# A graph network on one core: norms woven into the products around them

## The reference, cut to what matters

```python
x = _layernorm(x + _L0_gnn_ref(x, ...), axis=-1)   # two GCN convolutions
x = _layernorm(x + _L1_gnn_ref(x, ...), axis=-1)   # seg. means over dst and over src, then a GRU cell
x = _layernorm(x + _L2_gnn_ref(x, ...), axis=-1)   # three dense layers on [x, summed edge_attr, u], leaky relu
x = _layernorm(x + _L3_gnn_ref(x, ...), axis=-1)   # two SAGE convolutions
```

## Time and profile before

| | us |
|---|---|
| median of 3 runs | 1084.41 (1082.30 to 1086.23) |
| the profiled execution, its own time | 1082.45 |
| its span, first to last instruction | 1080.8 |
| mean granted PE clock in it | 0.938 |
| PE busy | 955.1 |
| DVE busy | 618.8 |
| ACT busy | 483.5 |
| POOL busy | 67.1 |

### The profile page before, as it was taken

How to read it: one execution, slowest core, us unless ns; L and a number is a source line. 1 busy time by engine, 2 the same in 40 slices (tenths; PEclk the granted TensorE clock), 3 DMA queues, 4 the chain that set the end, 5 groups by cost and what they waited for, 6 DMA issues and landing times.

```text
span 1080.8 us, 19631 instructions
## 1 busy us (share of the span) xinstructions
PE 955.1 (88%) x7324; PEld 831.5 (77%) x7324; DVE 618.8 (57%) x905; ACT 483.5 (45%) x787; POOL 67.1 (6%) x134
## 2 busy tenths in 40 slices
PE   7469999997799999759989899899699599999993
PEld 6469999997799799749978788544344399969982
DVE  3669999995544555645554455354623545415544
ACT  0135445444655566375557567322322523233311
POOL 1200000000000000200003244100000000000000
PEclk9989999999899999959989999899689689999997
DMA  9767777774000000000000000000000000000001
GB/s 268 140 148 170 169 164 170 162 168 99 2 0 0 1 1 0 20 0 0 0 2 0 0 1 0 1 1 8 17 0 1 0 1 0 1 1 1 0 0 60
DMA packets 168662, 48.00 MB, mean 44 GB/s; under 512 B 154948, under 2 KB 167268, under 8 KB 168593
## 3 DMA queue, kind: packets, MB, share of 16 engines
q1 hardware_dynamic: 155462, 44.96, 18.1%
q10 hardware_dynamic: 12012, 0.83, 0.8%
q0 software_dynamic: 1120, 1.29, 0.5%
HBM read 45.44 MB, written 8.02 MB: 49 GB/s over the span
## 4 chain that ended last, share of the span: by engine, by line
PE 82%; DVE 6%; ACT 4%; DMA 3%; issue 2%; SPq 2%; ACTq 0%; DVEq 0%
PE bank L1393 17%; PE bank L1394 16%; PE bank L1336 11%; PE bank L1326 7%; PE bank L1488 4%; PE bank L1481 4%; PE bank L1489 3%; PE bank L1564 2%; PE bank L1527 2%; DMA lists_d<-in_src 2%; ACT wb L715 2%; PE bank L1553 2%; PE bank L1528 2%; DVE tmp L1010 1%; PE bank L1552 1%
## 5 line engine op out<-in xcount | busy, mean ns | idle before, releaser
L1393 PE MATMUL bank<-stage,f_hi 125*128 125x392 f32 x1000 | 348.1, 348 | 36.9 <-DVE f_lo L1054 21.3
L1394 PE MATMUL bank<-stage,f_lo 125*128 125x392 f32 x1000 | 345.8, 346 | 0.0
L1393 PEld LDWEIGHTS bank<-stage,f_hi 125*128 125x128 f32 x1000 | 192.0, 192 | 40.0 <-issue 23.3
L949 DVE CAST stage<-counts 125x2352 fp32r (+1 forms) x120 | 165.4, 1381 | 97.4 <-PE bank L1394 97.0
L1394 PEld LDWEIGHTS bank<-stage,f_lo 125*128 125x128 f32 x1000 | 191.9, 192 | 0.0
L688 ACT ACTIVATE stage<-counts 125x1568 fp32r x80 | 107.7, 1346 | 179.2 <-PE bank L1394 179.2
L1336 PE MATMUL bank<-tmp,wb 128*65 128x25 f32 x2000 | 130.3, 219 | 8.3 <-DVE tmp L901 8.3
L1336 PEld LDWEIGHTS bank<-tmp,wb 128*65 128x65 f32 x2000 | 127.1, 142 | 8.5 <-DVE tmp L901 8.5
L632 ACT ACTIVATE counts<-bank 125x500 uint8<-125x500 f32 x188 | 87.0, 536 | 43.4 <-PE bank L1326 42.9
L753 ACT ACTIVATE stage<-bank 125x500 fp32r<-125x500 bf16 x150 | 87.6, 588 | 37.4 <-PE bank L1481 29.1
L878 DVE TENSOR_TENSOR xT<-xT,tmp 128x2560 bf16<-128x2560 bf16 (+1 forms) x63 | 92.8, 1473 | 1.2 <-ACT rowb L612 1.2
(11 more groups left out here) (196 smaller groups left out, 972.4 us busy)
## 6 DMA issues: line engine op xcount, KB each, us to landing
wb<-in_edge_attr SPq DMA_DIRECT2D x125, 256.0 KB, 3.6
lists_d<-in_dst SPq DMA_DIRECT2D x1, 3104.0 KB
lists_d<-in_src SPq DMA_DIRECT2D x1, 3104.0 KB
wa<-in_x SPq DMA_DIRECT2D x1, 1562.5 KB
out<-wb SPq DMA_DIRECT2D x6, 250.0 KB
xT<-in_dst SPq DMA_DIRECT2D x63, 4.0 KB, 3.3
xT<-in_dst ACTq DMA_DIRECT2D x62, 4.0 KB, 3.0
wb<-in_L_gnn_w_ih SPq DMA_DIRECT2D x1, 384.0 KB, 3.6
```

Source lines behind the costliest of these rows:

```text
L949: nc.vector.tensor_copy(set_buffer(u, m), counts[:, SETS[u][0]:sum(SETS[u]), chunk(pair * 2 + off)]).then_inc(s["set_d_ready"], 1)
L1393: mm(bank[h][:, 0:CH], f_hi[:, first + k, :], rhs[:, k, :], start=(first + k == 0), stop=False)
L1394: last = mm(bank[h][:, 0:CH], f_lo[:, first + k, :], rhs[:, k, :], start=False, stop=(first + k == HI - 1))
```

## The change

Norm 0 is written out piece by piece: ACT widens sets 1 and 3 of sum 2's first chunk between the groups, DVE scales groups 4 to 6 and widens set 4 before its last low parts. DVE squares `rowb`, a chunk at a time, inside sum 2; POOL's squaring is gone. Sums 2 and 3 are written out without loops on ACT and DVE.

The gates use one bank each (0 to 3), and PE waits for each bank's reader in the chunk before. Norm 1 has three parts (groups 0 to 2, 3 and 4, 5 and 6). Its groups are transposed from banks 4 to 6 behind gate chunks 2, 3, 4, 6 and 7 and between the first layer products; all go back through bank 7 and ACT. The layers' products use banks 0 and 1, 2 and 3, and 4. Norm 2, also in three parts, begins behind layer chunk 2. L2's weights but `l2w2` move to `wl3` and are loaded when L3's were; `l2w2` is loaded when the gate products that read its place are done; L3's weights follow the last result. The statistics of norms 1 and 2 have a small tensor of their own, `n_small`.

```diff
-        NORM_BANK = ((2, 3, 4, 5, 6, 7, 1), (0, 1, 2, 3, 4, 5, 6), (0, 1, 2, 3, 4, 5, 6), (0, 1, 4, 5, 6, 7, 2))
-        BACK_BANK = ((4, 5, 6, 7, 4, 5, 6), (7, 0, 1, 2, 3, 4, 5), (4, 5, 6, 7, 4, 5, 6))
...
+        NORM_BANK = ((2, 3, 4, 5, 6, 7, 1), (4, 5, 6, 4, 5, 6, 5), (5, 6, 7, 5, 6, 7, 2), (0, 1, 4, 5, 6, 7, 2))
+        BACK_BANK = ((4, 5, 6, 7, 4, 5, 6), (7, 7, 7, 7, 7, 7, 7), (4, 5, 6, 7, 4, 5, 6))
+        PARTS_OF = ((0, 2, NGR), (0, 3, 5, NGR), (0, 3, 5, NGR), (0, 4, NGR))
+        ACT_SCALES = ((0, 1, 2, 3), (0, 1, 2), (3, 4), (0, 2, 4, 6))
...
             sp.wait_ge(s["y_made"], NC)
+            sp.dma_start(l2w1x, p["L2_gnn_w1"][0:D, :]).then_inc(s["l2w_in"], 16)
+            sp.dma_start(l2w1a, p["L2_gnn_w1"][D:D + DE, :]).then_inc(s["l2w_in"], 16)
+            sp.dma_start(l2w1u, p["L2_gnn_w1"][D + DE:256, :]).then_inc(s["l2w_in"], 16)
+            sp.dma_start(l2w3, p["L2_gnn_w3"].rearrange("(k p) n -> p k n", k=2)).then_inc(s["l2w_in"], 16)
+            sp.wait_ge(s["gates_done"], 4 * NC - 2)
+            sp.dma_start(l2w2, p["L2_gnn_w2"].rearrange("(k p) n -> p k n", k=2)).then_inc(s["l2w_in"], 16)
+            sp.wait_ge(s["l2_y"], NC)
...
-            pool.wait_ge(s["norm_t"], NGR)
-            nc.gpsimd.tensor_tensor(rowb[:, :], rowb[:, :], rowb[:, :], ALU.mult).then_inc(s["rowb_sq"], 1)
...
-            norm_to_sources(0, 2)
-            neighbour_sum(2)
+            deviations(0, 0)
+            scaled(0, 0)
+            high_part(0, 0)
+            scaled(0, 1)
+            high_part(0, 1)
+            widen_set(2, 0, 0, 1)
+            deviations(0, 1)
+            scaled(0, 2)
+            high_part(0, 2)
+            scaled(0, 3)
+            high_part(0, 3)
+            high_part(0, 4)
+            widen_set(2, 0, 0, 3)
+            high_part(0, 5)
+            high_part(0, 6)
+            rest_of_sum(2, ((0, 0, 1), (0, 0, 3)))
...
+                act.wait_ge(s["gates_done"], 4 * c + 1)
                 if c >= 1:
                     act.wait_ge(s["gate_y"], c)
+                nc.scalar.activation(tmp[:, 0, :], bank[0][:, 0:CH], ACT.Sigmoid, bias=cols[:, C_BR:C_BR + 1]).then_inc(s["gate_r"], 1)
+                act.wait_ge(s["gates_done"], 4 * c + 2)
+                nc.scalar.activation(tmp[:, 1, :], bank[1][:, 0:CH], ACT.Sigmoid, bias=cols[:, C_BZ:C_BZ + 1]).then_inc(s["gate_z"], 1)
+                if c == 6:
+                    scaled(1, 0)
+                    scaled(1, 1)
+                if c == 7:
+                    scaled(1, 2)
+                    keep_back(1, 0)
                 act.wait_ge(s["gate_t"], c + 1)
                 nc.scalar.activation(tmp[:, 3, :], tmp[:, 2, :], ACT.Tanh, bias=cols[:, C_BIH + 2:C_BIH + 3]).then_inc(s["gate_n"], 1)
+                if c == 5:
+                    deviations(1, 0)
             nc.scalar.activation(small[:, 0:1], mean_w[:, :], ACT.Sqrt)
...
+            act.wait_ge(s["bu_made"], 1)
+            keep_back(1, 1)
+            hidden(0, 0)
+            keep_back(1, 2)
             deviations(1, 1)
...
+            for c in range(NC):
+                if c + 1 < NC:
+                    hidden(0, c + 1)
+                if 1 <= c <= 4:
+                    keep_back(1, c + 2)
+                if c == 6:
+                    deviations(2, 0)
+                if c == 7:
+                    high_part(2, 0)
+                    high_part(2, 1)
+                hidden(1, c)
+                if c == 0:
+                    deviations(1, 2)
+            high_part(2, 2)
+            deviations(2, 1)
+            act.wait_ge(s["l2_y"], NC)
+            widen_set(3, 0, 0, 1)
+            scaled(2, 3)
+            high_part(2, 3)
+            deviations(2, 2)
+            scaled(2, 4)
+            high_part(2, 4)
+            widen_set(3, 0, 0, 3)
+            high_part(2, 5)
+            high_part(2, 6)
+            rest_of_sum(3, ((0, 0, 1), (0, 0, 3)))
...
+            def neighbour_sum(q, dest, more=None, then=None, unrolled=False, first_last=True, squared=False):
...
+                    c = pair * 2 + off
+                    if squared:
+                        nc.vector.tensor_tensor(rowb[:, chunk(c)], rowb[:, chunk(c)], rowb[:, chunk(c)], ALU.mult).then_inc(s["rowb_sq"], 1)
+                        dve.wait_ge(s["rowb_sq"], c + 1)
                     dve.wait_ge(s["set_d_used"], pair * 6 + (24 * q + 3 * off + 3 + 2))
...
+                        if first_last or h or not isinstance(pair, int) or pair:
+                            conv(q, pair, h, 4)
...
+                if unrolled:
+                    for t in range(NC // 2 - 1):
...
+            statistics(0, 0)
+            statistics(0, 1)
+            variances(0, 0)
+            statistics(0, 2)
+            statistics(0, 3)
+            scales(0, 0)
+            for k in (4, 5, 6):
+                statistics(0, k)
+            variances(0, 1)
+            low_part(0, 2, 0)
+            conv(2, 0, 0, 2)
+            low_part(0, 2, 1)
+            scales(0, 1)
+            scaled(0, 4)
+            low_part(0, 2, 2)
+            scaled(0, 5)
+            scaled(0, 6)
+            low_part(0, 2, 3)
+            conv(2, 0, 0, 4)
+            for k in (4, 5, 6):
+                low_part(0, 2, k)
...
+            neighbour_sum(2, wa, unrolled=True, first_last=False, squared=True)
...
             for c in range(NC):
+                dve.wait_ge(s["gates_done"], 4 * c + 3)
                 dve.wait_ge(s["gate_r"], c + 1)
+                nc.vector.scalar_tensor_tensor(tmp[:, 2, :], bank[3][:, 0:CH], cols[:, C_BHH + 2:C_BHH + 3], tmp[:, 0, :], ALU.add, ALU.mult).then_inc(s["gate_h"], 1)
+                if c in (3, 4, 5):
+                    statistics(1, c - 3)
+                if c == 5:
+                    variances(1, 0)
+                    dve.wait_ge(s["l2_bias"], 1)
+                    nc.vector.tensor_tensor(cols[:, C_L2BU:C_L2BU + 2], cols[:, C_L2B1:C_L2B1 + 2], bank[7][:, 0:2], ALU.add).then_inc(s["bu_made"], 1)
+                if c == 6:
+                    scales(1, 0)
+                if c == 7:
+                    statistics(1, 3)
+                dve.wait_ge(s["gates_done"], 4 * c + 4)
+                dve.wait_ge(s["gate_h"], c + 1)
+                nc.vector.tensor_tensor(tmp[:, 2, :], tmp[:, 2, :], bank[2][:, 0:CH], ALU.add).then_inc(s["gate_t"], 1)
...
+            statistics(1, 4)
+            variances(1, 1)
             leaky(0, 0)
+            scales(1, 1)
+            scaled(1, 3)
+            statistics(1, 5)
+            scaled(1, 4)
+            leaky(0, 1)
             for c in range(NC):
+                if c >= 1 and c + 1 < NC:
                     leaky(0, c + 1)
+                if c == 0:
+                    statistics(1, 6)
+                    variances(1, 2)
+                if c in (3, 4, 5):
+                    statistics(2, c - 3)
+                if c == 5:
+                    variances(2, 0)
+                if c == 6:
+                    scales(2, 0)
+                    scaled(2, 0)
+                    scaled(2, 1)
+                if c == 7:
+                    scaled(2, 2)
+                    low_part(2, 3, 0)
+                    low_part(2, 3, 1)
+                    statistics(2, 3)
+                    statistics(2, 4)
+                    variances(2, 1)
                 leaky(1, c)
+                if c == 0:
+                    scales(1, 2)
+                    scaled(1, 5)
+                    scaled(1, 6)
+                if c in (1, 2):
+                    conv(3, 0, 0, 2 * c - 2)
                 dve.wait_ge(s["l2_y"], c + 1)
...
+            low_part(2, 3, 2)
+            scales(2, 1)
+            statistics(2, 5)
+            statistics(2, 6)
+            variances(2, 2)
+            low_part(2, 3, 3)
+            scales(2, 2)
+            scaled(2, 5)
+            scaled(2, 6)
+            conv(3, 0, 0, 4)
+            for k in (4, 5, 6):
+                low_part(2, 3, k)
+            neighbour_sum(3, wa, unrolled=True, first_last=False)
...
+                earlier = [b for b in range(k) if NORM_BANK[i][b] == NORM_BANK[i][k]]
+                if earlier:
+                    wait_scaled(pe, i, earlier[-1])
...
+                if c:
+                    pe.wait_ge(s["gate_r"], c)
+                input_gates(c, 0)
+                if c:
+                    pe.wait_ge(s["gate_z"], c)
+                input_gates(c, 1)
+                if c:
+                    pe.wait_ge(s["gate_h"], c)
+                mm(bank[3][:, 0:CH], wt["whh2"], xT[:, chunk(c)], start=True, stop=True).then_inc(s["gates_done"], 1)
+                if c:
+                    pe.wait_ge(s["gate_t"], c)
+                input_gates(c, 2)
+                if c in (2, 3, 4, 6, 7):
+                    k = (2, 3, 4, 6, 7).index(c)
+                    node_group(1, k, "gate_y", chunks_for[k])
+                if c == 4:
+                    pe.wait_ge(s["l2w_in"], 64)
+                    for m in range(2):
```

(29 more changed lines are left out.)

314 lines of the change are left out of this document (121 added, 193 removed).

## The result

The changed kernel takes 1042.11 us (median of four executions, 1041.20 to 1043.62) against 1085.32 us (1082.3 to 1086.31) for the kernel before, run on the same chip: a ratio of 0.9609, with a 95% interval of 0.9586 to 0.9631. The forecast was 1046 us, range 1039 to 1061.

The account below looks back on a forecast made before the run. PE was taken to bound the kernel, busy 88% of 1080.8 us, with gains only where it waits or its clock is down. Terms of 8.4 + 13.7 + 1.0 + 15.4 = 38.5 us off the 1084.41 us median gave 1046 us, range 1039 to 1061.

Parts of the forecast that it names:

- Term 1: Norm 0 into sum 2: sum 2's first chunk ends at 478 us against 486.4 before, -8.4 us.
- the lower end: Lower bound of the forecast: no new wait brings PE's clock down, 1046 - 7 = 1039 us.
- Between, at nothing: Items costed at no gain or loss, among them the two unrolled sums and the moved weight loads.
- Term 2: Gates and norm 1: the first product of the three layers starts at 759.0 instead of 772.7, -13.7 us.
- Term 3: Three-layer products: 8.4 us regained by arriving warm, spent again on transposes and late results; 73.1 us against 74.1, -1.0 us.
- Term 4: Norm 2 into sum 3: first chunk ends 12.9 us after the last result instead of 28.4, -15.4 us.
- Cold products: Rival: the clock falls behind gate chunk 6 and stays down in the first layer products; 1058 us, chance 0.15.
- Queues bind the starts: Rival: ACT's and DVE's strict orders still hold up the first chunks of sums 2 and 3; 1054 us, chance 0.21.
- Single banks serialise: Rival: in gates and layers PE waits every step for the previous step's reader, losing 70 us; 1116 us, chance 0.03.

Follow-up runs that it names:

- square_only: The kernel before, with only POOL's squaring of rowb replaced by DVE's eight pieces inside sum 2: 1075.6 us, ratio 0.9939.
- pool_square: The changed kernel with POOL's squaring of rowb put back behind norm 0's last transposes: 1050.1 us, ratio 0.9696.
- warm0: The changed kernel with 12 extra products, result unused, in PE's wait between norm 0's transposes and sum 2: 1042.0 us, ratio 0.9616.
- early_scales: The changed kernel with DVE's scales of norm 1's first part moved to step 5's end and a dummy sigmoid behind the square root: 1038.1 us, ratio 0.9574.
- norm1_behind: The changed kernel with norm 1's first five groups taken out of the gates and put behind them: 1051.0 us, ratio 0.9706.
- rows128: The kernel before, with 128-row products in place of the 64-row edge products in the layers' first two chunks: 1072.4 us, ratio 0.9892.

## Why the prediction was right, point by point

*Term 1, norm 0 into sum 2: forecast -8.4, measured -10.9 us (35.9 to 25.0).* The start was right (462.2 forecast, 462.01 measured). What was mis-sized is the fourth set's wait: I let the last low parts come at 474.7, and they were done at 473.2, so the wait was 1.6 us instead of 2.2. The clock did not fall behind it, where I had taken a value near the one for a fallen clock (the lower end then counts 1.7 us for this term although I had added only 1.1 of them). square_only and pool_square show that POOL's squaring, priced at 4.9, is worth 5.7 alone and 7.1 in the new order. The cause was right, both by removal and by putting it back. DVE's eight pieces cost nothing: DVE is idle for half of a sum, and a chunk still takes 8.93 us. warm0 shows that the clock in the first products costs nothing here.

*Between, at nothing: measured +1.1 us.* From sum 2's first chunk to the first gate product the changed kernel is 1.1 us longer, 0.4 of it a longer wait behind sum 2 (2.48 us for 2.09) and most of the rest a clock that came back later at the edge sums. That the unrolled sums gain nothing is borne out: a chunk takes 8.93 us in both kernels.

*Term 2, gates and norm 1: forecast -13.7, measured -13.7 us (80.1 to 66.4).* The 1.7 us wait was there to the tenth, with the cause that was named, the late load and the late scales: early_scales removes it. norm1_behind gives back 8.5 of the 13.7; it keeps the bank layout of the changed kernel, and leaves groups 5 and 6 among the layers, so the other 5.2 us lie in these parts, which no run took apart.

*Term 3, the layers: forecast -1.0, measured -1.0 us, partly for a wrong reason.* Arriving warm was to give 8.4 us back, and the first 16.9 us did run at 1.00. But the cause, idle time before them, was incomplete: norm1_behind arrives cold and has its clock back in 1.7 us. The long slow stretch also needed the two chunks of products with 128 and 64 rows in turn (rows128 ends it after 3.1 us). In the changed kernel transposes stand between the first and the second of these chunks; whether that alone would have been enough no run shows. The 73.1 us follow as 8 x 7.37 + 5.5 + 3.3 + 3.4 + 2.0 = 73.2, not from the changes that are listed against 74.1, which give 75: 1.9 us of the transposes had lain between these products already. The two waits were 3.0 and 3.1 us (forecast 3.3 and about 3.4), the slow results 2.66 and 2.27 (forecast 2.53 twice).

*Term 4, norm 2 into sum 3: forecast -15.4, measured -16.1 us (28.7 to 12.6).* Forecast +12.9 us after the last result, measured 12.6. This is the largest term, and no run takes norm 2 back out of the layers; the traces alone show it. In this stage PE's idle time falls from 13.2 us to 0.7, and its work at 0.50 from 10.3 us to 4.6.

*The rivals.* Cold products: its condition did not occur, since the clock stayed at 1.00 through the wait behind chunk 6 (687.8 to 810.7), and norm1_behind refutes its price for a clock that is down at the layers' start. Queues bind the starts: in the mild sense true, as warm0 shows, but the 8 us it would have cost did not appear. Single banks serialise: PE shows no wait for a gate's bank in any chunk. The terms summed to 38.5 us, the stages to 40.6 (35.9 + 206.1 + 80.1 + 74.0 + 28.7 less their values after); the difference is term 1's 2.5 and term 4's 0.7 less the 1.1 in between. The medians differ by 43.2 us, because the profiled execution of the kernel before was one of its fastest.
